# Loading the first banded chunk of x ahead of step 0, the two others two steps sooner

## The reference

```
x = x + causal_conv16(x, taps)      # depthwise: channel c, tap k from cond[k, c]
h = cond                            # initial state, 16 x 512
for t in range(256):
    gi = x[:, t] @ W_ih + b_ih      # 512 x 1536
    gh = h @ W_hh + b_hh
    r = sigmoid(i_r + h_r); z = sigmoid(i_z + h_z)
    n = tanh(i_n + r * h_n)
    h = (1 - z) * n + z * h
    out[:, t] = x[:, t] + h
```

## Time and profile before

| What | Value |
|---|---|
| median of 3 runs | 983.01 us |
| profiled execution, its own time | 983.77 us |
| span of its profile | 982.0 us |
| TensorE busy | 970.7 us (99% of the span) |
| VectorE busy | 880.2 us (90%) |
| ScalarE busy | 511.6 us (52%) |
| GpSimd busy | 565.9 us (58%) |
| small loads of x (L308) | 24 transfers of 64 KB |
| bands (L302) | 12 transfers of 64 KB |
| load of L338 | one transfer of 376 KB |

### The profile page before, as it was taken

The page is one execution under the profiler, slowest core; times in us unless marked ns, Lnnn a source line. Parts: engine busy times, 40 slices in busy tenths (PEclk is TensorE's granted clock), DMA queues, the critical chain, the costliest instruction groups (busy, mean ns, idle before and its releaser), DMA issues.

```text
span 982.0 us, 62625 instructions
## 1 busy us (share of the span) xinstructions
PE 970.7 (99%) x26066; PEld 788.8 (80%) x26068; DVE 880.2 (90%) x3075; ACT 511.6 (52%) x2154; POOL 565.9 (58%) x1597
## 2 busy tenths in 40 slices
PE   8999999999999999999999999999999999999997
PEld 5898888888788888888888888888888888888775
DVE  7879999999999999999999999999999988888555
ACT  4334555555555555555555555555555555555543
POOL 6556665655655555555555555656556555555542
PEclk9999999999999999999999999999999999999999
DMA  8731001010010101101010010100101000000000
GB/s 304 74 42 36 25 16 34 16 41 20 20 33 16 38 20 30 30 13 37 16 36 25 17 37 12 41 20 20 37 14 36 14 25 26 12 28 5 23 16 13
DMA packets 67596, 32.37 MB, mean 33 GB/s; under 512 B 44528, under 2 KB 65648, under 8 KB 67312
## 3 DMA queue, kind: packets, MB, share of 16 engines
q1 hardware_dynamic: 66880, 28.25, 11.4%
q10 hardware_dynamic: 432, 0.11, 0.0%
HBM read 19.86 MB, written 8.49 MB: 29 GB/s over the span
## 4 chain that ended last, share of the span: by engine, by line
PE 96%; DVE 2%; DMA 0%; issue 0%; POOL 0%; ACT 0%; POOLq 0%; DVEq 0%; SPq 0%
PE pg L811 67%; PE pcv L615 8%; PE pg L605 8%; PE pg L615 4%; PE pcv L625 4%; PE pcv L635 3%; PE pg L595 1%; DVE x L1014 1%; DMA xs<-x 0%; PE pcv L605 0%; PE pcv L826 0%; DVE x L1004 0%; DVE gt L1076 0%; POOL nzh L572 0%; DVE hp L1101 0%
## 5 line engine op out<-in xcount | busy, mean ns | idle before, releaser
L811 PE MATMUL pg<-whh,hp 128*32 128x192 f32 x16384 | 716.3, 326 | 5.9 <-DVE hp L1101 3.5
L811 PEld LDWEIGHTS pg<-whh,hp 128*32 128x32 f32 x16384 | 521.9, 110 | 137.2 <-DVE hp L1101 14.4
L1032 DVE SCALAR_TENSOR_TENSOR pcv<-xb,cnd,pcv 128x256 f32<-128x256 f32 (+2 forms) x588 | 315.1, 536 | 6.9
L984 ACT ACTIVATE rz<-gt 128x64 f32<-128x64 f32 x512 | 136.2, 266 | 302.6 <-DVE gt L1076 274.9
L572 POOL TENSOR_TENSOR nzh<-rz,hp 128x32 f32<-128x32 f32 x512 | 158.7, 310 | 218.3 <-ACT rz L984 216.6
L1076 DVE STREAM_TRANSPOSE gt<-pg 128x128 f32<-128x128 f32 x512 | 162.1, 317 | 49.8 <-PE pg L811 42.2
L989 ACT ACTIVATE nzh<-an 128x32 f32<-128x32 f32 x512 | 121.1, 236 | 127.1 <-DVE an L1088 127.1
L1101 DVE TENSOR_TENSOR_SCAN hp<-zcp,nzh 128x96 f32<-128x96 f32 x512 | 173.1, 338 | 12.0 <-ACT nzh L989 9.4
L1088 DVE TENSOR_TENSOR_SCAN an<-rz,gn 128x64 f32<-128x64 f32 x512 | 149.9, 293 | 26.3 <-ACT rz L984 25.9
L986 ACT ACTIVATE zcp<-gt 128x32 f32<-128x32 f32 x512 | 111.0, 217 | 0.0
L1080 DVE STREAM_TRANSPOSE gn<-pg 128x64 f32<-128x64 f32 x512 | 107.2, 209 | 0.0
(11 more groups left out here) (110 smaller groups left out, 879.9 us busy)
## 6 DMA issues: line engine op xcount, KB each, us to landing
xb<-x SPq DMA_DIRECT2D x96, 94.0 KB, 2.0
out<-x SPq DMA_DIRECT2D x60, 128.0 KB, 1.8
wih<-w_ih SPq DMA_DIRECT2D x4, 768.0 KB, 8.1
whh<-w_hh SPq DMA_DIRECT2D x4, 512.0 KB, 12.3
xw<-x SPq DMA_DIRECT2D x24, 64.0 KB, 3.5
whh<-w_hh SPq DMA_DIRECT2D x4, 256.0 KB, 13.8
xb<-x SPq DMA_DIRECT2D x16, 62.0 KB, 1.9
tz<-taps SPq DMA_DIRECT2D x12, 64.0 KB, 3.5
```

Of the source, the lines that this page charges most:

```text
L811: i = pe.matmul(pg[t // 2 % Q][f][D * j:D * (j + 1), 0:IN], hp[:, t % 2, 2 * c + 1 - t % 2:2 * c + 3 - t % 2, :, 1].rearrange("p u b -> p ...
L984: act.activation(rz[:, f, :, :, 1].rearrange("p g (c b) -> p (g c) b", b=B), gt[:, f, :, u], ACT.Sigmoid).then_inc(s_rz[f], 1)
L1032: dve.scalar_tensor_tensor(x1_of(c, a, b)[:, lo:hi] if lag == K - 1 else sums, xx[:, c, (K - 1 - lag) * B + lo:(K - 1 - lag) * B + hi], cn ...
```

## The change

`BAND` and `WINDOWS` lose their entry for chunk 1, and those of chunks 2 and 3 are two steps lower. The eight loads and four bands of chunk 1 are issued in front of the loop, behind the last whh transfer and ahead of the wait for the third whh chunk and of the load of L338. The loop runs over chunks 2 and 3 only. No instruction is added or removed; TensorE's, VectorE's, ScalarE's and GpSimd's programs are the same. For chunk 1 the loads now come before the bands, and so also before the two waits of the first band. Chunk 2 has its bands at step 0 and its loads in steps 1 and 2, chunk 3 at step 2 and in 3 and 4.

```diff
@@ -216,8 +216,8 @@
         TURNED = {1: 5, 2: 7, 3: 10}
         EARLY = {1: 2, 2: 2, 3: 2, 4: 3, 6: 3, 8: 2, 9: 2}
         SPANS = [(a - W2 - 5, a - 5) for a, _ in LONG]
-        BAND = {1: 0, 2: 2, 3: 4}
-        WINDOWS = {1: (1, 3), 2: (3, 5), 3: (5, 7)}
+        BAND = {2: 0, 3: 2}
+        WINDOWS = {2: (1, 3), 3: (3, 5)}
         PIECES = 4
 
         FIRST = [(lag, c) for lag in range(FEW) for c in range(C - 1)]
@@ -334,11 +334,15 @@
             for c in range(C):
                 sp.dma_start(whh[:, c, F:], w_hh[:, c, 0:2 * F]).then_inc(s_whh[c], 16)
                 sp.dma_start(whh[:, c, 0:F], w_hh[:, c, 2 * F:]).then_inc(s_whh[c], 16)
+            for q in range(2 * G):
+                load(BANDED[0], q)
+            for g in range(G):
+                band(BANDED[0], g)
             sp.wait_ge(s_whh[C - 2], 32)
             sp.dma_start(xb[1][:, 0, :], x[:, 0, B:(W2 + TB) * B]).then_inc(s_xe, 16)
             for t in range(T):
                 sp.wait_ge(s_h[0], t + 1)
-                for c in BANDED:
+                for c in BANDED[1:]:
                     if t == BAND[c]:
                         for g in range(G):
                             band(c, g)
```

## The result

The changed kernel takes 990.09 us (median of 6 runs, 989.28 to 990.88) against 983.25 us for the kernel before on the same chip (982.98 to 983.42): a ratio of 1.0069, 95% interval 1.0059 to 1.0078. It is slower by 6.8 us, where 2.8 were forecast, and lies outside the range. The profiled execution took 989.69 us, its span is 988.0.

The account below looks back on a forecast made before the run. TensorE, busy 99% of the span, was taken to bound the kernel. Earlier loads gain 0 and the stall costs 2.8 us: 983.01 + 2.8 = 985.8 us, range 982.9 to 988.2.

Parts of the forecast that it names:

- The mechanism of the stall and its sign: Step 1: VectorE waits for the large x load behind twelve small transfers, TensorE idles before step 3; slower by 2.8 us.
- no value in the earlier loads: Turning multiplications at L826: TensorE never waits for the moved loads, so their being earlier gains 0.
- Every later stretch as long as before: After the stall between steps 2 and 3, TensorE's work was to keep its durations, with no further loss.
- The landing of xe: When the large early load of x for chunk 0 (L338) arrives: forecast 32.7 us, against 24.5 before.
- The way by SyncE: Landing by issue pace, 0.887 us per small transfer: large x load issued at 29.8, landing at 33.2 us.
- The way by the packets: Landing by DMA engines: twelve transfers take 8.4 us after whh ends, large x load lands at 32.3 us.
- the middle, 32.7: Landing time in us taken for the large x load, between the two estimates of 32.3 and 33.2.
- my own formula: TensorE's stall before step 3: large x load's landing minus 29.66, less 0.3 us slack; 2.7 to 2.8 us.
- The clock: Rival, chance 0.06: TensorE's clock falls in the stall, one step's 3.9 us of matmuls take twice as long; 989.7 us.
- my high bound of 5.1 us: Largest loss: no small transfer accepted before 21.06, large x load lands at 35.1; 988.1 us.
- whh delayed: Rival, chance 0.05: small packets mix with the weights, step 0 begins late; up to 991.4 us, with half 987.2.
- my single term of 2.8 us: The only loss summed: idle TensorE between steps 2 and 3, added to the median of 983.01 us.

Follow-up runs that it names:

- xe first: Changed kernel with the large early load of x for chunk 0 (L338) and its wait moved back ahead of chunk 1's twelve small transfers: 983.18 us, ratio 0.9999.
- all doses: Changed kernel with 4 bands, 8 loads or 24 small transfers ahead of the large x load: 983.96, 984.95, 1000.56 us; with 12, the change itself: 990.09.
- the run with the others sooner: Kernel before with only chunks 2 and 3 two steps sooner, chunk 1's transfers left in the loop: 985.71 us, ratio 1.0028.
- The fill: Changed kernel with twelve multiplications of zeros in TensorE's program at the end of step 2: 987.81 us.
- the two kernels with the reader later: VectorE's sixteen early convolution instructions start in step 3 instead of step 1: changed kernel 985.96 us; control, the kernel before with the same shift, 985.33 us.

## Why the prediction was wrong

*Right.* The mechanism of the stall and its sign: no value in the earlier loads (xe first, 0.9999); xe behind twelve transfers; VectorE stalled in step 1; TensorE idle between steps 2 and 3. "Every later stretch as long as before" was not right: step 3's multiplications took 4.36 us. The rule of the Trainium skill (DMA: Bandwidth & Descriptors, Queues, rings and completion order), by which one ring's descriptors are taken in order, agrees with all doses, and with xe in ScalarE's queue, which landed at 25.8 us. It is hardly put to the test: 9.1 of the 9.6 us by which xe lands late lie before its issue, in SyncE, and only 0.5 behind it.

*The landing of xe, mis-sized by 1.4 us.* The way by SyncE gave 29.8 for the issue and 33.2 for the landing; measured 30.19 and 34.1, 0.4 late by the issue and 0.5 by the transfer (3.9 us for 3.4). The way by the packets gave 32.3, and taking the middle, 32.7, lost another 0.5. It was the middle of a limit (the DMA engines at full rate) and of an account of the queue that issues at its measured pace. The slower of two stages in a row decides, and the slower was SyncE. With 34.1 in my own formula, 34.1 - 29.96, the stall comes to 4.1 us; measured 4.0 to 4.2.

*The clock: the step that failed.* I wrote "My stall of 2.8 us is shorter than that idle time, so I expect the clock to stay at 2.4 GHz", and gave the fall 0.06. The stall was 4 us, and the clock fell. The landing is part of that: at 33.2 the stall is 3.2 us, hardly shorter than the 3.3 us between TensorE's last work at 978.1 and the fall at the end of the kernel before, and at my high bound of 5.1 us the same row spoke for a fall; yet the bound of 988.1 left it out. But the comparison itself was no ground for a forecast. The runs show no such order of idle times: the clock fell behind a wait of 1.86 us with eight loads ahead of xe, stayed up through one of 1.88 us with xe in ScalarE's queue (TensorE resumed at 23.60; 1.00 from 21 to 24 us) and through 2.50 us in the run with the others sooner, and fell 4.7 us after TensorE's last work with 24 transfers ahead. What decides is not shown here. The fill shows what the fall is worth, 2.3 us. In the profile it cost 1.9, not the 3.9 that I put down for it, since it fell only after work had resumed and came back within the step. That my rival with the clock ends at 989.7, near the measured 990.09, is luck: its stall was 1.2 us too small and its clock 2.0 us too large.

*whh delayed: partly right.* I gave it 0.05 as a case by itself. It came beside the stall, with 0.2 us in the profile of the changed kernel and 0.6 us between the two kernels with the reader later. It is small, but it belongs to the sum; no run shows by what it comes about.

*The sum.* In the place of my single term of 2.8 us stand 4.0 (stall) + 1.9 (clock) + 0.2 (whh) = 6.1 by the steps, against 6.0 by the spans and 5.9 by the two profiled executions (989.69 - 983.77). The other 0.9 us of the difference of the medians: the profiled execution of before lay 0.5 above its median, and that of after 0.4 below its own, since three of six runs belong to the group with the lower mean clock (0.996). I have no profile of one of those; that a longer low stretch makes the group is only argued.

## What to carry to other kernels

- A transfer issued early is free only for its own reader. List what stands behind it in the same queue, when each of those is read, and add the pace of issue (here 0.9 us for 1024 runs of 64 B) for each one that goes ahead; where two stages limit the landing, take the slower, not the middle.
- A stall of TensorE can cost more than itself: here 4.0 us of it brought 1.9 us of lower clock on top. The length of one idle time after which the clock was seen to fall does not tell whether it will. Price the fall inside the range, and not as a remote rival; if the stall can't be avoided, useless multiplications in it win back part.
- If loads are to go early, put the large transfer with the earliest reader, and what it waits for, first. That made the changed kernel equal to the one before, and no faster.

## What the runs showed of the hardware

- Small-piece transfers that are issued while the weights fill the DMA engines hold SyncE: eight loads took 17.2 us from 9.2 on, against 7.1 us once whh was through. One single issue lasted 8.4 us (the tile's rows of the changed kernel: min, median and max in ns):

```profile
L308 SPq DMA_DIRECT2D xw<-x x24: 563/772/8416, 9.2 to 51.7; - x24
```

- The granted clock fell 1.1 us after TensorE had resumed work in the changed kernel. In the kernels with eight loads ahead and with the reader later it fell in step 0, behind waits of 1.86 and 2.21 us for the last whh chunk in a stretch that had other gaps; with xe in ScalarE's queue it stayed at 2.4 GHz behind a wait of 1.88 us in the same place.
- Small packets queued behind large ones on the same queue went with a later release of the engine that waits for the large ones, by 0.1 to 1.2 us, although all large ones had been issued first and, in the kernel looked at, their packets had ended a microsecond before.
